# A decoder layer with a mixture of experts: three plans for the expert slots, the first once two batches are routed

## The reference, cut to what matters

```python
x = layernorm(x + attn(x))              # 4 batches x 512 rows, width 256, 16 heads
x = layernorm(x + xattn(x, ctx))        # 64 context rows per batch
x = layernorm(x + ffn(x))

def ffn(x):                             # 8 experts, 2 for each row
    probs = softmax(x @ router_w.T)
    vals, idx = top_k(probs, 2)
    for e in range(8):
        w = sum(where(idx == e, vals, 0))
        out += w * (gelu(x @ w1[e].T) @ w2[e].T)     # hidden width 1024
```

## Time and profile before

| | |
|---|---|
| median of three runs | 821.5 us (818.32 to 822.62) |
| profiled execution | 821.51 us, its span 819.7 us |
| TensorE matmul busy | 726.1 us (89%) |
| VectorE, ScalarE, GpSimd busy | 334.0, 287.5, 223.1 us |
| chain that ended last | TensorE 77%, VectorE 8%, DMA 5%, ScalarE 4% |
| mean granted TensorE clock | 0.931 |

### The profile page before, as it was taken

One profiled execution on the slowest core, in us unless ns is written; L12 is line 12 of the kernel. 1 busy time (PEld: TensorE's weight loads), 2 busy tenths in 40 slices (PEclk: granted clock), 3 DMA queues, 4 the chain that ended last, 5 costly groups with the idle time before them and its releaser, 6 DMA issues.

```text
span 819.7 us, 11598 instructions
## 1 busy us (share of the span) xinstructions
PE 726.1 (89%) x3964; PEld 469.8 (57%) x3965; DVE 334.0 (41%) x762; ACT 287.5 (35%) x525; POOL 223.1 (27%) x280
## 2 busy tenths in 40 slices
PE   6899999999999689997977947989999999999970
PEld 3323233322224365554555436969999999999960
DVE  3687777689982654533536151300000000000004
ACT  2246656667764433434332312111111111111112
POOL 2211111111115421102041341543333333333322
PEclk9869999999999989999987667989999999999995
DMA  5974124424432160001020077666666665566616
GB/s 160 182 168 93 17 66 91 79 61 96 79 115 81 49 208 1 1 1 51 1 52 0 7 200 238 170 134 165 173 182 185 190 169 164 157 179 180 171 11 205
DMA packets 58910, 92.84 MB, mean 113 GB/s; under 512 B 13841, under 2 KB 45298, under 8 KB 57331
## 3 DMA queue, kind: packets, MB, share of 16 engines
q1 hardware_dynamic: 50355, 83.86, 36.5%
q0 software_dynamic: 8512, 8.44, 6.6%
HBM read 75.94 MB, written 17.86 MB: 114 GB/s over the span
## 4 chain that ended last, share of the span: by engine, by line
PE 77%; DVE 8%; DMA 5%; ACT 4%; issue 3%; POOL 2%; SPq 1%; POOLq 0%; DVEq 0%; ACTq 0%
PE ps L1888 16%; PE ps L1899 16%; PE ps L1568 7%; PE ps L1559 7%; PE ps L1493 6%; PE ps L1597 3%; DVE nmx L1061 2%; PE ps L1511 2%; PE ps L1724 2%; PE ps L1683 2%; ACT probs L859 2%; PE ps L1714 2%; PE ps L1580 1%; PE ps L1717 1%; PE ps L1672 1%
## 5 line engine op out<-in xcount | busy, mean ns | idle before, releaser
L859 ACT ACTIVATE probs<-ps 128x512 f32<-128x512 f32 x256 | 136.0, 604 | 102.7 <-PE ps L1559 102.1
L1061 DVE TENSOR_REDUCE nmx<-ps 128x1 f32<-128x512 f32 x256 | 159.7, 680 | 15.7 <-PE ps L1493 15.0
L1888 PEld LDWEIGHTS ps<-xtT,w1c 128*128 128x128 f32 x1248 | 146.2, 193 | 2.4 <-issue 0.5
L1888 PE MATMUL ps<-xtT,w1c 128*128 128x128 f32 x1248 | 146.8, 276 | 0.4 <-issue 0.4
L1899 PE MATMUL ps<-wexp,hidT 128*128 x624 | 144.0, 385 | 0.7 <-issue 0.7
L1899 PEld LDWEIGHTS ps<-wexp,hidT 128*128 128x128 f32 x624 | 117.7, 194 | 16.3 <-issue 1.6
L1454 DVE TENSOR_SCALAR yw<-ps,mt 128x256 f32<-128x256 f32 x39 | 18.9, 484 | 256.3 <-PE ps L1899 254.1
L1022 ACT ACTIVATE hidT<-ps 128x1024 f32<-128x1024 f32 x39 | 39.9, 1023 | 225.8 <-PE ps L1888 207.2
L804 POOL DMA_INDIRECT acc<-yw,mt x39 | 62.0, 1589 | 170.7 <-DVE yw L1454 163.9
L1493 PE MATMUL ps<-kst,qst 96*128 96x512 bf16 x256 | 98.7, 409 | 4.5 <-DVE nmx L1061 3.1
L1559 PE MATMUL ps<-qst,kst 99*128 99x512 bf16 x256 | 94.0, 391 | 1.0 <-ACT probs L859 0.7
(11 more groups left out here) (204 smaller groups left out, 780.8 us busy)
## 6 DMA issues: line engine op xcount, KB each, us to landing
w1c<-in_w1T SPq DMA_DIRECT2D x39, 1024.0 KB
wexp<-in_w2T SPq DMA_DIRECT2D x8, 1024.0 KB
kst<-scrk SPq DMA_DIRECT2D x48, 128.0 KB, 6.9
qst<-scrq SPq DMA_DIRECT2D x8, 384.0 KB, 4.8
xTb<-in_xT SPq DMA_DIRECT2D x4, 512.0 KB, 7.6
qst<-scrq SPq DMA_DIRECT2D x8, 256.0 KB, 5.4
xr<-in_x SPq DMA_DIRECT2D x4, 512.0 KB, 5.1
x2d<-xr SPq DMA_DIRECT2D x4, 512.0 KB, 4.0
```

Source lines behind the costliest of these rows:

```text
L859: act.activation(probs[n % 8][:, :], ps[:, 4 + n % 3, :], ACT.Exp).then_inc(s_exp, 1)
L1061: dve.tensor_reduce(nmx[w % 2][:, k:k + 1], ps[:, ring_bank("max", w, k), :], AX.X, ALU.max, negate=True).then_inc(s_mfree, 1)
L1888: mm = pe.matmul(ps[:, 2 * (j % 2) + f // 4, f % 4 * P:(f % 4 + 1) * P], w1c[j % 2][:, k * FF + f * P:k * FF + (f + 1) * P], xtT[j % 2][:, ...
```

## The change

- There are three plans: 9 slots once batches 0 and 1 are counted, 8 more once batch 2 is, and the other 22 at the end. One function `make_plan(n)` replaces the two. The number of slots stays 39.
- TensorE counts batches 0 and 1 (`count(1, 1, 128)`) within the last cross-attention, behind the second `turn_x` of batch 2, and VectorE makes the first plan there. The second plan stands behind the last `add_residual` of batch 3 instead of between its `norm_o`s.
- SyncE's loads of the first `mt` groups and of `w1c` for slots 0 and 1 move ahead of the loads of experts 2, 3 and 5 and of the store of batch 2's rows. They wait for the first plan and for the metadata of batches 0 and 1.
- GpSimd issues the gathers of slots 0 to 2 ahead of `scatter_metas(2)` and of `rstd` of batch 3; batch 3's metadata scatters move from behind scatters 1 and 2 to behind scatters 4 and 5.
- TensorE transposes slot 0 between steps 1 and 2 of the last end, and makes its hidden product in four parts behind steps 2, 3, 4 and 5. `turn_x`, logits, positions and count of batch 3 move behind later slots.
- PSUM banks and SBUF places are dealt anew: hidden products in banks 5, 6 and 2, 3, out products in 1 and 0, slot transposes in 4, `turn_x` of batch 3 in 7. `xt` and `xtT` lie where weights of phase 0 and of the q projection were, so their clearing waits for the last sum of phase 0.

```diff
-EARLY = 2 * (NB - 1) * S // P - NE + 1
+def full_tiles(batches):
+    return 2 * batches * S // P - NE + 1
+PLANS = (0, full_tiles(NB - 2), full_tiles(NB - 1), NSLOT)
...
+    HID_BANK, OUT_BANK, TURN_BANK = (5, 2), (1, 0), 4
...
+        sp.wait_ge(s_planned, 1)
+        for b in range(2):
+            sp.wait_ge(s_disp[b], 16 * 2 * QT)
         load_metas(0)
+        sp.wait_ge(s_on, tiles_of(1, 0) + QT)
         load_w1(0, 0)
         load_metas(1)
+        sp.wait_ge(s_on, tiles_of(1, 1) + QT)
         load_w1(1, 1)
+        sp.wait_ge(s_pv2, NU * NB)
+        for e in (2, 3, 5):
+            load_expert(e)
+        store_x2(2)
         load_metas(2)
         store_x2(NB - 1)
         for t in range(2, NSLOT):
             load_w1(t, t)
...
         for t in range(3):
             gather(t)
+        scatter_metas(2)
+        rstd_of(1, 3)
...
             scatter(t)
-            if 1 <= t <= 2:
-                scatter_metas(NB - 1, (t - 1,))
+            if 4 <= t <= 5:
+                scatter_metas(NB - 1, (t - 4,))
...
+        def make_plan(n):
+
+            last = n == len(PLANS) - 2
+            lo, hi = PLANS[n], PLANS[n + 1]
+            done_of = done_early[:, 0:NE]
+            dve.wait_ge(s_cnt, n + 1)
+            plan_step(dve.tensor_copy(cnt[:, :], ps[0:1, 7 if last else 1, 128:128 + NE]))
...
+            slot_plan(lo, hi, done_early[:, 0:1])
...
-            plan_early()
             norm_o(1, 3, 2)
             add_residual(1, 3, 0)
             norm_o(1, 3, 3)
             for t in range(1, QT):
                 add_residual(1, 3, t)
+            make_plan(1)
...
+        end_step(1, 3, 0)
+        positions(2)
+        end_step(1, 3, 1)
+        pe.wait_ge(s_exp2, NP * NB)
+        turn_tile(0, 0, 0)
+        end_step(1, 3, 2)
+        count(2, 1, 128)
+        pe.wait_ge(s_w1c[0], 16)
+        pe.wait_ge(s_xtT, 1)
+        hidden_part(0, (0, 1))
+        end_step(1, 3, 3)
+        hidden_part(0, (2, 3))
+        turn_tile(1, 1, 0)
+        end_step(1, 3, 4)
+        hidden_part(0, (4, 5))
+        end_step(1, 3, 5)
+        hidden_part(0, (6, 7)).then_inc(s_mm1, 1)
+        pe.wait_ge(s_o2, NE_TILES)
         pe.wait_ge(s_y, NE_TILES)
         hidden(1, 1, 0)
+        turn_tile(2, 0, 1)
+        pe.wait_ge(s_planned, 2)
         pe.wait_ge(s_we, 16 * NE)
         expert_out(0, 0)
+        turn_x(1, 3, 0)
+        hidden(2, 2, 1)
```

More of the change, by code:

```diff
@@ L162, in decoder_layer @@
     room = sb("room", NE, F32, R_CONST, 1)
+    left = sb("left", NE, F32, R_CONST, 1)
     spare = sb("spare", NE, F32, R_CONST, 1)
@@ L345, in decoder_layer @@
     s_slot = sem("slots_ready")
-    s_disp = [sem(f"metas_scattered_{i}") for i in range(2)]
+    s_disp = [sem(f"metas_scattered_{b}") for b in range(NB)]
     s_cnt = sem("count_matmul_ready")
@@ L782, in known @@
         def known(t):
-            return (NB - 1) * S if t < EARLY else T
+            return S * (NB - 2 + sum(t >= lo for lo in PLANS[1:3]))
         def checked(t):
@@ L1002, in _ @@
         last_cross()
-        for t in range(QT):
-            copy_o2(1, 3, t)
-        normalise(1, 3)
         def copy_xtT(t, j):
             act.wait_ge(s_tpx, t + 1)
[L1009 to L1016, removed]
+            act.activation(xtT[j % 2][:, :], ps[:, TURN_BANK, 0:D], ACT.Copy).then_inc(s_xtT, 1)
         def gelu(t, j):
@@ L1021, in gelu @@
                 act.wait_ge(s_mm2, t - 1)
-            act.activation(hidT[j % 2][:, :], bank(2 * (j % 2), 2), ACT.Gelu).then_inc(s_h, 1)
-        gelu(0, 0)
-        with act.Fori(0, NSLOT // 4) as i:
+            act.activation(hidT[j % 2][:, :], bank(HID_BANK[j % 2], 2), ACT.Gelu).then_inc(s_h, 1)
+        copy_o2(1, 3, 0)
+        copy_o2(1, 3, 1)
+        copy_xtT(0, 0)
+        copy_o2(1, 3, 2)
+        copy_o2(1, 3, 3)
+        copy_xtT(1, 1)
+        act.activation(ahead[:, 2:3], ahead[:, 1:2], ACT.Gelu)
+        gelu(0, 0)
+        normalise(1, 3)
+        gelu(1, 1)
+        copy_xtT(2, 2)
+        copy_xT(1, 3, 0)
+        gelu(2, 2)
+        copy_xT(1, 3, 1)
+        copy_xtT(3, 3)
+        gelu(3, 3)
+        router_exp(3)
+        copy_xtT(4, 4)
+        gelu(4, 4)
+        copy_xtT(5, 5)
+        with act.Fori(1, NSLOT // 4) as i:
             for j in range(4):
@@ L1847, in last_cross @@
             turn_x(1, 2, 1)
+            count(1, 1, 128)
             exp2_tile(3, 4)
@@ L1863, in _ @@
         last_cross()
-        end_step(1, 3, 0)
-        positions(2)
-        end_step(1, 3, 1)
-        count(2, 6, 0)
-        for step in range(2, QT + 2):
-            end_step(1, 3, step)
         def turn_tile(t, j, turn):
@@ L1876, in turn_tile, with hidden_part @@
             for k in range(KD):
-                mm = pe.transpose(ps[:, 6, k * P:(k + 1) * P], xt[j % 2][:, k * P:(k + 1) * P], identf[:, :])
+                mm = pe.transpose(ps[:, TURN_BANK, k * P:(k + 1) * P], xt[j % 2][:, k * P:(k + 1) * P], identf[:, :])
             mm.then_inc(s_tpx, 1)
+        def hidden_part(j, parts):
+            for f in parts:
+                for k in range(KD):
+                    mm = pe.matmul(ps[:, HID_BANK[j % 2] + f // 4, f % 4 * P:(f % 4 + 1) * P],
+                                   w1c[j % 2][:, k * FF + f * P:k * FF + (f + 1) * P], xtT[j % 2][:, k * P:(k + 1) * P],
+                                   start=(k == 0), stop=(k == KD - 1))
+            return mm
         def hidden(t, j, turn):
@@ L1885, in hidden @@
                 pe.wait_ge(s_h, t - 1)
-            for f in range(KF):
-                for k in range(KD):
-                    mm = pe.matmul(ps[:, 2 * (j % 2) + f // 4, f % 4 * P:(f % 4 + 1) * P],
-                                   w1c[j % 2][:, k * FF + f * P:k * FF + (f + 1) * P], xtT[j % 2][:, k * P:(k + 1) * P],
-                                   start=(k == 0), stop=(k == KD - 1))
-            mm.then_inc(s_mm1, 1)
+            hidden_part(j, range(KF)).then_inc(s_mm1, 1)
         def expert_out(t, j):
```

135 lines of the change are left out of this document (62 added, 73 removed).

## The result

| | before | after |
|---|---|---|
| median | 822.06 us (818.32 to 823.37, 4 runs) | 811.79 us (810.67 to 814.1, 4 runs) |
| profiled execution, span | 821.51, 819.7 us | 814.1, 812.3 us |
| TensorE, VectorE, ScalarE, GpSimd busy | 726.1, 334.0, 287.5, 223.1 us | 721.6, 338.6, 290.2, 223.8 us |

The ratio is 0.9891 [0.9853, 0.993]: 9.0 us faster by it, 10.3 us by the medians. The forecast was 809.7 us with a range of 802 to 817. The profiled execution of after is the slowest of its four, so the two traces, laid side by side, differ by only 7.4 us.

The account below looks back on a forecast made before the run. TensorE was taken as the bound, nine tenths busy except around the wait for the first gather. Slot 5 comes 18.4 us earlier, less 6.6 at gather 8, net 11.8: 821.5 - 11.8 = 809.7 us, own range 806 to 813, wider 802 to 817.

Parts of the forecast that it names:

- the two holes that were forecast: TensorE waits for slot 2's `w1c` (4.0 us) and slot 8's gather (3.63 us), each followed by 3.0 us of low clock.
- A: Rival: one of the two TensorE holes does not open, another 6.6 to 7 us go, 803 us; chance 0.20.
- C: Rival: DMA engines set the time before hidden product 2, about 8.4 MB to move; at 200 GB/s 818 us; chance 0.06.
- D: Rival: slower, as late slot 0 data delays end steps, `rstd`, store and third `w1c`; 826 us; chance 0.04.
- B: Rival: clock stays at half through the last end's steps, 7.4 us become 14.8; 816 us; chance 0.15.
- Slot 0's rows at 469.7: First gather lands at 469.7 us, with batch 1's metadata taking 2.0 us to land (473.6 by the long end).
- End steps and four parts done at 485.3: Last end on TensorE: 7.4 us of work after 477.9 at full clock, waits covered; last out-projection at 484.4 instead of 487.1.
- GpSimd decides when `rstd` starts: Batch 3's `rstd` starts at 486.3, when GpSimd is free of eight metadata scatters; the last sum would allow 485.9.
- The plan's wait before out product 0: Slot 0's out product waits for the second plan, ready at 489.8: a new wait of 0.7 to 1 us.
- The hole for `w1c` of slot 2: Before hidden product 2 TensorE waits 4.0 us for the load behind batch 3's store, plus 3.0 us of low clock.
- Slot 5 at 525.2: Start of slot 5's hidden product, the fixed point of TensorE's order: 525.2 against 543.6, 18.4 us early.
- The hole of 6.6 us recurs at gather 8: Slot 5's gather wait moves to slot 8 with the moved scatters: 3.63 us plus 3.0 of low clock, bounds 0 to 6.6.

Follow-up runs that it names:

- the second profile of the changed kernel: The changed kernel run again without any edit: median 812.35 us (4 runs), ratio 0.988.
- without parts: The changed kernel with slot 0's hidden product made whole behind the last end step instead of in four parts: 809.3 us, ratio 0.9853.
- The run with pairs: The changed kernel with batch 3's metadata scatters two behind each of slot scatters 4 to 7, not four behind 4 and 5: 809.2 us, ratio 0.9832.
- eight gathers more: The changed kernel with eight further gathers into unused buffers behind batch 2's metadata scatters, ahead of `rstd`: 823.1 us (1 run).
- arithmetic in place of the run: The changed kernel with eight 128x512 GpSimd additions where batch 2's metadata scatters were, and those scatters behind `rstd`: 808.55 us (1 run).
- The three without parts: The changed kernel with slot 0's product whole: alone 809.3 us; with third `w1c` ahead of the store 807.15; also batch 3's scatters dealt over slots 3 to 8, 803.4.

## Why the prediction was right, and where it was not

The direction, the time within 2.1 us and the mechanism in the main were right. Slot 0's work now fills the seam, the long wait for its gather is gone, and the two holes that were forecast did open, each with a low clock behind it. Rivals A (no hole), C and D did not happen. B had a part in it: the clock was 0.93 and 0.81 where I had put 1.0, but as the effect of a wait, not its cause. By steps:

- **Slot 0's rows at 469.7: wrong, 473.6.** The term is the landing of batch 1's metadata, for which I took 2.0 us between ends of 1.7 and 5.9. It took 4.5 us on quiet queues (issue ended 461.2, SyncE went on at 465.8), and the last scatter was issued 1.6 us later than before. The `mt` read (1.74 us) and the gather (4.12 us) cost what the rows said. TensorE waited 2.35 us for it, since it had come to the seam 2.0 us earlier than before (468.2 against 470.2 at the first turn of the last end); in the second profile of the changed kernel it came at 470.5 and didn't wait, and both start slot 0's transposes at 473.76. The fixed time of about 2 us in the Trainium skill (DMA: Bandwidth & Descriptors, Anatomy of one DMA — SWDGE (gpsimd) path) is thus less than half of what this transfer took, and weights in the queues are not needed to explain most of the long row of before.
- **End steps and four parts done at 485.3, last out-projection at 484.4: the step that failed.** It ended at 491.8. I wrote that the waits between steps "lie behind the parts". Of the 2.10 us wait in the earlier trace rows I took it that more TensorE work would cover it; 1.5 us of it (482.96 to 484.49) were no latency but the hold under GpSimd's run of scatters, and it grew to 5.01 us as the run now ends 4.6 us later (486.43 against 481.83). The out-projection behind it ran at half clock too (2.04 us in place of 1.03); short gaps between the steps are the rest. Everything up to slot 5 is late by this: last statistics 492.9 against 485.7 forecast (7.2), `rstd` 493.3 against 486.3 (7.0), `w1c` 504.8 against 497.7 (7.1).
- **GpSimd decides when `rstd` starts: wrong in the changed kernel** (VectorE was last, GpSimd idle for 5.91 us), right without parts, where `rstd` starts 0.03 us after the scatters (483.48).
- **The plan's wait before out product 0: right in size, by luck.** 0.7 to 1 us forecast, 1.16 measured. But TensorE was done at 496.94 and the plan's last cast ends at 497.01, so the plan itself was 0.07 us late; the other 1.1 us, from the cast to the matmul that has its expert's number from the plan, the forecast did not have. (The row names ScalarE's `hidT`; that is slot 1's, and slot 0's ended at 494.2.) The first plan cost nothing (15 instructions of before, 17 now, beside idle time), as forecast.
- **The hole for `w1c` of slot 2: 7.0 forecast, 4.4 measured** (2.61 of wait; the product took 5.47 us against 3.73). The wait is smaller because TensorE itself came later, which saves nothing; the 1.3 us less of low clock do.
- **Slot 5 at 525.2: 530.7**, 5.5 later: the 7.1 above, less 1.3 of low clock that slot 2 didn't cost, and 0.3 on the way. The earlier arrival at the seam has no part in the 12.9 us: the wait for slot 0's rows used it up, and the second profile of the changed kernel, which arrives at 470.5, has slot 5 at 530.53. (The arrival, in a part that is nearly the same in all, lies between 465.3 and 472.5 in the fourteen traces.)
- **The hole of 6.6 us recurs at gather 8: place and cause right, 4.7 measured**: 2.93 and 0.41 us of waits and 1.4 of low clock. The run with pairs shows that the four scatters ahead of the gather were its cause. One wait came that I had not seen: 0.93 us at 535.45, with 0.43 behind it, for the gather of slot 6, which was issued at 527.22 and took 8.19 us where others took 4 to 5. The chain leads its issue back to ScalarE, where the router's Exp now falls between two Gelus:

```profile
519.09 1.28 ACT L935 ACT_TABLE_LOAD   x1
...
523.80 1.28 ACT L1029 ACT_TABLE_LOAD   x1 [2.91 <-PE ps L1921]
```

These two rows alone don't make the wait: the second profile has both (518.92 and 523.63) and issues the gather at 527.05, and TensorE doesn't wait there. What made this one transfer longer isn't shown; `w1c` was moving beside it.

The rhythm of the slots behind the holes, for the product that starts at 602.64 + 7.24 = 609.88 before:

```profile
603.05 3.73 PE L1902 MATMUL ps<-xtT,w1c 128*128 128x128 f32 x32
```

It is 6.8 us earlier: the 12.9 of slot 5, less 4.7 at slot 8 and 1.4 at slot 6. The spans differ by 7.4. The forecast had 18.4 less 6.6. Between the profiled executions the gain is thus 4.4 us below the forecast, and the hold is the largest part of it. In the medians it is 10.3. The second profile of the changed kernel (span 810.4, 1.9 us shorter) shows what such a difference can be made of, and it isn't the hold. The hold is shorter there, 6.07 us on VectorE instead of 7.30, and the last out-projection starts 1.2 us earlier (488.55). But the third `w1c` then took 6.80 us instead of 5.74 and TensorE waited 3.74 us for it, so slot 5 starts at 530.53, 0.17 us earlier. What is missing is the wait at slot 6.

So the time is better than its working, and that is partly luck. One term was too small by 7 us. Against it stand the two low clocks, too large by 1.3 and 1.6 (1.4 in place of 3.0). The way from 4.4 us in the profiled execution to 2.1 us in the median is the spread between executions of one kernel.

**What stays open.** By what path a run of indirect transfers makes TensorE's signals late. The records of semaphore updates give this much: between 440 and 520 us, in all fourteen traces, the updates that come over 0.3 us behind the row that makes them are TensorE's alone, and none of the recorded ones of VectorE and ScalarE. (Some updates have no record.) The one ahead of the last out-projection is 5.31 us late in the changed kernel and 15.38 us with eight gathers more, the longest of all; with arithmetic in place of the run, two are 5.68 and 5.30 us late under the moved run. That also fits what the rows show of TensorE: it was not seen held itself, it is the one that is heard late.

In eleven traces, before's among them, VectorE's last held wait ends 1.9 to 2.8 us behind the last transfer's start, and it moves and grows with the run. The three without parts are different: one has its sums unheld and a Gelu held to 4.4 us behind, the others have signals that are late by 0.8 to 1.9 us. The first sum comes through the run unheld in every trace, and in four traces a held copy of ScalarE's goes on before the last transfer starts. All this is read from profiled executions; no run shows whether the signals are as late without the profile.

The Trainium skill (Trainium Architecture — The Big Picture, What this means for kernel authors) names one thing that VectorE and GpSimd share, a pair of ports under an exclusive lock. It doesn't fit: ScalarE, which has no part in it, was held too, and 8 us of GpSimd arithmetic held nobody (one run).

## What to carry to other kernels

A wait whose releaser the profile does not name ("remote", "unknown queue") is not slack that more work covers: look what GpSimd issues at that time, and where its run of indirect transfers ends. Keep such runs short or put them where VectorE and ScalarE don't wait for TensorE. Here leaving a product whole, moving one load and breaking up one run gave nearly as much again as the change (812 to 803 us). When a chain is shortened, compare each next load's place in its queue: the third `w1c` behind a store was worth about 4 us by the medians, and cost nothing to move.

## What the runs showed of the hardware that I had not expected

- Under a run of 9 to 18 indirect transfers (1.26 to 1.30 us each) TensorE's signals were late, by up to 15.4 us behind the row of the matmul: with 18, VectorE stood idle for 15.98 us and ScalarE for 13.19 us. 8 us of arithmetic on GpSimd did nothing of the kind.
- A scatter of 128 pieces of 8 bytes to HBM took 4.5 us from the end of its issue until it was seen, on quiet queues (under 5 GB/s from 461 to 466).
- From a plan's last VectorE instruction to the first matmul that uses it, TensorE took 1.0 to 1.1 us (497.01 to 498.11, and 488.29 to 489.30 in the run with arithmetic).
- A change of ScalarE's function between Gelu and Exp cost 1.28 us each way, and two more of them appeared because batch 3's Exp moved from ahead of the first Gelu to between two.
